# Second layer of a two-layer sequence model on one core: step sizes started ahead of the gates, row numbers counted on by ScalarE, and another order of work on the way to the sorted experts

## What is computed

```python
x_ssm, res = jnp.split(x @ W_in.T, 2, axis=-1)           # 512 and 512 channels
x_ssm = silu(causal_conv4(x_ssm) + b_conv)
dt = softplus(x_ssm @ W_dt.T + b_dt)                     # the step sizes
B_C = (x_ssm @ W_x.T)[..., 16:]                          # 16 states
def step(h, inp):                                        # 2048 steps, 512 x 16 states
    h = exp(dt_t[:, :, None] * A) * h + dt_t[:, :, None] * B_t[:, None, :] * x_t[:, :, None]
    return h, h.sum(-1) + D * x_t
y = scan(step) * silu(res)                               # silu(res): the gates
x = x + y @ W_out.T
# then two groups of 32 experts, top 2 of each: route, sort rows by expert,
# grouped SwiGLU, weighted sum back to the tokens
x = x + (group0(layernorm(x)) + group1(layernorm(x))) / 2
```

## Time and profile before

| | us |
|---|---|
| median of 3 runs | 4872.82 (4868.73 to 4875.76) |
| the profiled execution, whole | 4861.3 |
| its span, first to last instruction | 4859.5 |
| layer 1, from the first product L1456 (2499.1) to the end of the last (4167.0) | 1667.9 |
| from there to the first expert tile (4256.6) | 89.6 |
| experts, to the end | 602.9 |

### The profile page before, as it was taken

One profiled execution on the slowest core, in us unless ns is written; L12 is line 12 of the kernel. 1 busy time (PEld: TensorE's weight loads), 2 busy tenths in 40 slices (PEclk: granted clock), 3 DMA queues, 4 the chain that ended last, 5 costly groups with the idle time before them and its releaser, 6 DMA issues. The chain is left out here.

```text
span 4859.5 us, 59293 instructions
## 1 busy us (share of the span) xinstructions
PE 4278.9 (88%) x19350; PEld 2834.2 (58%) x19350; DVE 3722.3 (77%) x5916; ACT 2516.5 (52%) x4871; POOL 3037.6 (63%) x1970
## 2 busy tenths in 40 slices
PE   5689999999999999998988889888988888499993
PEld 1355555555556655565655566555655665388883
DVE  6887777778788878775149988888988898555676
ACT  1344334334333434433468777777777777155552
POOL 3455555555555545554158889888888888555552
PEclk7899999999999999999999999999999999699997
DMA  4233332333332333333112221111222111496787
GB/s 146 80 107 104 109 100 92 110 98 111 109 104 90 105 105 104 105 109 100 39 67 75 80 73 70 70 69 69 86 87 75 69 67 68 162 248 209 260 282 278
DMA packets 304193, 545.54 MB, mean 112 GB/s; under 512 B 31504, under 2 KB 148496, under 8 KB 294928
## 3 DMA queue, kind: packets, MB, share of 16 engines
q1 hardware_dynamic: 276240, 466.09, 29.5%
q0 software_dynamic: 27648, 75.67, 4.3%
HBM read 422.72 MB, written 118.92 MB: 111 GB/s over the span
## 5 line engine op out<-in xcount | busy, mean ns | idle before, releaser
L1456 POOL TENSOR_TENSOR c_dbx<-c_dtx,c_Brep 128x1024 f32<-128x1024 f32 x512 | 1200.5, 2362 | 167.8 <-DVE c_hs L1474 57.5
L876 POOL TENSOR_TENSOR a_kv<-a_rk,a_kv 128x512 f32<-128x512 f32 x512 | 807.7, 1589 | 402.9 <-DMA a_kv<-v_rows 402.6
L1474 DVE TENSOR_TENSOR_SCAN c_hs<-psum,c_carry,c_dbx 128x512 f32<-128x512 f32 x768 | 937.4, 1266 | 120.6 <-ACT psum L1463 68.0
L885 DVE TENSOR_TENSOR_SCAN a_S<-a_decay,a_carry,a_kv 128x513 f32<-128x513 f32 x512 | 795.1, 1553 | 185.4 <-POOL a_kv L876 94.4
L1463 ACT ACTIVATE psum<-c_dt,c_cols 128x512 f32<-128x512 f32 x1024 | 698.9, 689 | 402.6 <-DVE c_hs L1474 398.0
L802 POOL TENSOR_TENSOR a_hid_e<-a_hid_e,a_g_rep 128x512 f32<-128x512 f32 x256 | 386.7, 1513 | 773.3 <-ACT a_hid_e L791 596.9
L1490 PEld LDWEIGHTS psum<-ident,c_hs 128*128 128x128 f32 x4096 | 488.2, 144 | 394.5 <-DVE c_hs L1474 217.5
L1490 PE MATMUL psum<-ident,c_hs 128*128 128x128 f32 x4096 | 612.0, 282 | 114.1 <-DVE c_hs L1474 109.9
L891 DVE TENSOR_TENSOR a_prod<-a_rk,a_S 128x512 f32<-128x512 f32 x512 | 547.3, 1069 | 68.4 <-PE psum L907 68.4
L783 PE MATMUL psum<-a_W_down,a_hid_e 128*128 128x256 f32 x2304 | 552.0, 385 | 52.7 <-POOL a_hid_e L802 28.5
L207 PE MATMUL psum<-a_xT,a_W_up 128*128 128x512 f32 x1152 | 559.2, 615 | 15.1 <-ACT a_hid_e L791 15.0
(11 more groups left out here) (271 smaller groups left out, 6777.5 us busy)
## 6 DMA issues: line engine op xcount, KB each, us to landing
a_kv<-v_rows SPq DMA_DIRECT2D x512, 256.0 KB
a_g_rep<-g_rows SPq DMA_DIRECT2D x256, 256.0 KB, 3.9
c_Brep<-b_rows SPq DMA_DIRECT2D x64, 1024.0 KB, 4.7
d_xs<-sorted_rows SPq DMA_DIRECT2D x320, 128.5 KB
d_w<-results SPq DMA_DIRECT2D x64, 512.0 KB, 11.4
d_w<-in_d_experts SPq DMA_DIRECT2D x32, 768.0 KB, 8.8
sorted_rows<-d_zeros SPq DMA_DIRECT2D x66, 128.5 KB, 6.2
a_xa<-in_L_attn_x SPq DMA_DIRECT2D x16, 512.0 KB, 4.7
```

What stands on the lines that cost most here:

```text
L876: m_kv[g] = pool.mark(nc.gpsimd.tensor_tensor(kv[:, g % NV, 1:C + 1], rk[slot][:, 1, hb, :], kv[:, g % NV, 1:C + 1], ALU.mult))
L885: m_scan[q] = dve.mark(nc.vector.tensor_tensor_scan(S[:, q % NS, :], decay[cq % 2][:, hb, :], kv[:, q % NV, :], carry[:, sq_:sq_ + 1], ALU ...
L1456: m_dbx[g] = m_dbx[g + 1] = pool.mark(nc.gpsimd.tensor_tensor(dbx[:, r:r + 2, :], dtx[slot][:, e, :].unsqueeze(1).broadcast_to([P, 2, C]), ...
L1474: m_scan[q] = dve.mark(nc.vector.tensor_tensor_scan(hs[:, q % NR, :], psum[:, DA + q % ND, :], dbx[:, q % NX, :], first, ALU.mult, ALU.add))
```

## The change

1. `m_done["xs", c]` is set before the gates, so `sizes` and `prepare` may begin in front of gates and B rows. `step_size(e)` for `e >= 1` waits until the B rows are written.
2. The row number is counted on by ScalarE: before the first pick right after the norm in `after_scan`, between the picks in `sort_rows`; ScalarE then waits for the landing of the first eight DMAs. The pause before it is shorter by two yields, and one yield stands behind it.
3. In chunk 15, a new generator `turned_early` transposes the first three of four blocks of the gated result and multiplies them with `W_out`; `last_product` adds the fourth.
4. For the last chunk the normed rows are copied (`again`, ScalarE) with the second row number (VectorE), and the 16 DMAs are issued group by group without a wait between the picks.
5. The expert phase fetches all 16 weight blocks of group 0 first, has the plan's constants on a semaphore of their own, issues the second pad from ScalarE's queue, waits for the plan only after that, waits for each group's last rows alone, and issues the third pad behind the first six row tiles.

```diff
@@ main
             for e0 in range(0, EB, 2):
                 yield from inner(e0)
                 yield
+            m_done["xs", c] = list(m_xs.values())
...
             yield from gates(2)
             m_done["gate", c] = m_gate[TL - 1]
-            m_done["xs", c] = list(m_xs.values())
@@ sizes
             def step_size(e):
+                while e >= 1 and not is_done(("stored", c)):
+                    yield
@@ after_scan
-            marks = m_done["y", c] = yield from transposed(gate[slot], yT, EB, m, y_free)
...
+            if c < NCH - 1:
...
+            else:
+                products = yield from last_product(c)
...
+            if c >= 2:
+                m_done["row", c] = act.mark(nc.scalar.activation(xn_[:, :, D], xn_[:, :, D], ACT.Identity, bias=two_chunks[:, 0:1]))
...
+            if c == NCH - 1:
+                act.after(m_done["scanned", c][0], m_done["scanned", c][1])
+                dve.after(m_done["scanned", c][0])
+                m_done["copied", c] = [act.mark(nc.scalar.copy(again[:, t, 0:D], xn_[:, t, 0:D])) for t in range(TL)]
+                m_done["copied", c].append(dve.mark(nc.vector.tensor_scalar(again[:, :, D], token_row[:, :], float(c * C * TOP + 1), None, ALU.add)))
@@ new
+        def turned_early(c):
+            marks = m_done["turned", c] = []
+            for e in range(EB - 1):
+                while not is_done(("gated", c, e)):
+                    yield
...
+                    m = nc.tensor.transpose(bank[:, t * P:(t + 1) * P], gate[c % 2][:, t, e * P:(e + 1) * P], ident[:, :])
...
+            while not is_done(("placed", c - 1)):
+                yield
...
+                    for e in range(EB - 1):
+                        nc.tensor.matmul(bank[:, t * D:(t + 1) * D], pre[:, e, at:at + P], W_out[:, e, :], start=(t == 0 and e == 0), stop=False, skip_group_check=True)
+                    yield
+            m_done["begun", c] = True
@@ sort_rows
-            if c >= 2:
-                pool.engine.wait_ge(s_sorted[c % 2], c // 2 * per_chunk)
-                m_row = pool.mark(nc.gpsimd.tensor_tensor(route.xn[c % 2][:, :, D], route.xn[c % 2][:, :, D], two_chunks[:, :], ALU.add))
+            m_row = m_done["row", c]
+            if c == NCH - 1:
+                pool.after_alone(*m_done["placed", c], *m_done["copied", c], m_row)
+                for g in range(GR):
+                    for k in range(TOP):
+                        for t in range(TL):
...
             for k in range(TOP):
                 if k:
-                    yield from pause(POOL_LAG)
-                    pool.engine.wait_ge(s_sorted[c % 2], c // 2 * per_chunk + per_chunk // TOP)
-                    pool.after_alone(pool.mark(nc.gpsimd.tensor_tensor(route.xn[c % 2][:, :, D], route.xn[c % 2][:, :, D], ones[:, 0:TL], ALU.add)))
+                    yield from pause(POOL_LAG - 2)
+                    act.engine.wait_ge(s_sorted[c % 2], c // 2 * per_chunk + per_chunk // TOP)
+                    m_row = act.mark(nc.scalar.activation(route.xn[c % 2][:, :, D], route.xn[c % 2][:, :, D], ACT.Identity, bias=ones[:, 0:1]))
+                    yield
+                    pool.after_alone(m_row)
@@ sorted_experts_phase
-        EARLY = 6
+        nc.sync.dma_start(plan, I["d_plan"]).then_inc(s_plan, 16)
         for n in range(EARLY):
             fetch_weights(0, n)
...
-        nc.sync.dma_start(plan, I["d_plan"]).then_inc(s_load, 16)
-        for n in range(EARLY, E // 2):
-            fetch_weights(0, n)
...
-        sp.after(m_plan, m_pad, m_zeros)
-        for block in range(PADS):
-            pad(block)
-        for slot in range(2):
-            sp.engine.wait_ge(s_sorted[0][slot], s_sorted[1])
+        sp.after(m_pad, m_zeros)
+        act.after(m_pad, m_zeros)
+        pad(0)
+        pad(1, nc.scalar)
+        sp.after(m_plan)
+        for sorted_sem, count in route.sorted:
+            sp.engine.wait_ge(sorted_sem, count)
         for j in range(AHEAD):
             fetch_rows(j)
+        pad(PADS - 1)
```

More of the change, by code:

```diff
@@ L1007, in layer1_phase @@
         s_sorted = [sem(f"sorted{i}") for i in range(2)]
+        s_last = [sem(f"last_of_group{g}") for g in range(GR)]
         NR, NX, DA, ND = 8, 6, 3, 3
@@ new lines, in last_product @@
+        def last_product(c):
+            e = EB - 1
+            while not is_done(("begun", c)):
+                yield
+            i, bank = yield from G.claim(pe)
+            pe.after(m_done["gated", c, e])
+            for t in range(TL):
+                m = nc.tensor.transpose(bank[:, t * P:(t + 1) * P], gate[c % 2][:, t, e * P:(e + 1) * P], ident[:, :])
+            act.after(pe.mark(m))
+            m_y = G.freed[i] = act.mark(nc.scalar.copy(pre[:, e, 0:C], bank))
+            pe.after(m_y)
+            products = []
+            for half, (i, bank) in enumerate(m_done["products", c]):
+                for t in range(2):
+                    at = (2 * half + t) * P
+                    m = nc.tensor.matmul(bank[:, t * D:(t + 1) * D], pre[:, e, at:at + P], W_out[:, e, :], start=False, stop=(t == 1), skip_group_check=True)
+                products.append((i, bank, pe.mark(m)))
+            return products
@@ L1672, in sorted_experts_phase @@
         pe, act, dve, pool, sp = L.pe, L.act, L.dve, L.pool, L.sp
-        s_load, s_out = sem("load"), sem("out")
+        s_load, s_plan, s_out = sem("load"), sem("plan"), sem("out")
         s_w = [sem(f"w{i}") for i in range(E // BLOCK)]
```

83 lines of the change are left out of this document (56 added, 27 removed).

## The result

The changed kernel takes 4884.58 us (median of 19 runs, 4876.77 to 4899.60), the kernel before 4875.76 us (19 runs, 4868.73 to 4886.45). The ratio is 1.0019, with a 95% interval of 1.0011 to 1.0026: 0.2% slower, where 4803 us and 1.5% faster had been forecast. The profiled execution took 4880.2 us, its span is 4878.4.

The account below looks back on a forecast made before the run. GpSimd, VectorE and TensorE were each taken as 89% busy in the loop, with GpSimd waiting for dtx. Loop 43 us plus way 27 us, together 70, took 4861.3 to 4791.3; plus 11.5 for the median, 4803 us, range 4768 to 4848.

Parts of the forecast that it names:

- The order of the step sizes: Loop: setting xs ahead of the gates removes GpSimd's 3.8 us dtx wait, less 1.35; gain 2.4 us a chunk.
- TensorE's order changes, its work doesn't: Loop, step sizes moved ahead of gates: TensorE only gets another order of the same work; no cost given.
- drift by a step a chunk: Loop background: earlier preparation could spread the router and make the sort stream slip one step a chunk; no cost given.
- rival C: Loop: step sizes hold banks, gates delay exponentials, losing 4.2 us a chunk; 4905 us in all, chance 0.07.
- The row numbers: Loop: two additions a chunk move from GpSimd to ScalarE, hidden there; 1.86 us a chunk off GpSimd.
- The ceiling of 6.0 us: Loop: chunk 1, without sorting, takes 100.5 us, so unhindered GpSimd buys at most 6.0 us a chunk.
- Rival A: Loop: VectorE keeps what GpSimd gives, dtx waits return as c_hs waits; loop gain 10, 4836 us, chance 0.18.
- The way: Last product to first expert tile: gains of 29.7 us, less 3, make 27 us, between 18 and 31.
- Last product: Way: with three quarters done early, last gate product to last sum falls from 12.1 to 4.4 us; gain 7.7.
- places to first tile: Way: from rows placed to first expert tile, 39.8 us becomes 19 to 21; gain 20.
- The 3 us taken off for ScalarE's wait: Way: 3 us deducted for late early products and ScalarE waiting for chunk 14's scatters ahead of the router's exp.
- Nothing in them changed: Experts: 320 tiles follow shifted at an even pace, staying at 603 us.

Follow-up runs that it names:

- e1: Kernel before with only the early order: xs set ahead of the gates, later step sizes behind the B rows; 4886.83 us, ratio 1.0050.
- e4: Changed kernel with only the early order taken back, xs set behind the gates again; 4838.87 us, ratio 0.9945.
- e6: Changed kernel with step sizes and the next input allowed from step 50 instead of 38; 4856.96 us, ratio 0.9961.
- e7: e4 with the two pauses of a chunk's first step size cut to one yield each; 4845.27 us, ratio 0.9929.
- e2: Kernel before with only the row numbers moved from GpSimd to ScalarE; 4867.90 us, ratio 1.0014.
- e11: e4 with norm statistics of one token block in four used for all, output not the reference's; executed once, loop 1647.1 us.
- e12: e7 and e8 together: e4 with short pauses and the third pad issued early by ScalarE; 4827.84 us, ratio 0.9931.
- e8: e4 with the third pad issued on ScalarE's queue ahead of the row tiles; ratio 0.9935.
- e5: Changed kernel with the next input's preparation held until all four gates are written; 4869.69 us, ratio 0.9983.
- e14: Kernel before with four banks for the background and two for the scans' exponentials, instead of three each; ratio 1.0071.
- e13: Changed kernel with four banks for the background and two for the scans' exponentials, instead of three each; ratio 1.0061.

## Why the prediction was wrong

**The order of the step sizes** was the step that failed. It said that the 3.8 us a chunk of waiting for `dtx` go, less 1.35 for the two operations that come ahead, and put the new order of TensorE's queue at nothing. Term forecast: +2.4 us a chunk; measured -1.9 alone (e1) and -2.7 beside the row numbers (after against e4). The wait did go (52.8 to 15.9 us). What stood in its place are waits that the same move makes: VectorE for the ranks' product, 28.2 us in e1 and 56.6 in e6, 1.2 before; GpSimd's products for scans, 80.6 for 37.1 us (e1); ScalarE with the gates' table loaded, 3.31 us in chunk 9; and the drift. The error was to price a wait by its length on the engine that waits, without asking what the moved operations would stand in front of. e6 and e7 remove it with no gain in a middle chunk, each at the price of a new wait, so how much of the 2.4 us was ever there stays open.

**"TensorE's order changes, its work doesn't"** passed over its first half. The order put products of step sizes between those of gates (3522.82 to 3532.06 above) and ahead of the ranks. The second half is true of the work, but not of its time: nearly the same records took 24 us more, at a granted clock of 0.96 for 0.99. Of the 32.0 us by which chunks 2 to 14 are longer than in the earlier trace rows, TensorE's busy time has 24.1. How much of those lies on the path isn't shown; in the ten us from 3528.5 TensorE is busy throughout and VectorE waits 6.87 us for it.

**The drift** was named ("drift by a step a chunk") and the banks were called what decides, but then rival C was turned down with the sentence that a held bank "makes a background stream give its turn away, it doesn't stop a queue". True, and it is how the order comes to drift: a stream that gives its turn away is written later, and from there the operations of five streams meet in other places in every chunk. C got the mechanism in part, the bank and the exponential behind a pair of gates, and missed its form: 2.5 us a chunk in a cycle of seven, not 4.2 in one collision. It had 0.07; the 1.9 us from which it was to decide was passed.

**The row numbers** were right in what they cost GpSimd (e2: 19.0 us of idle time and the additions gone) and wrong in what that is worth: 0.26 us a chunk, or 0.45 without chunk 2, not three quarters of 1.86. (Three quarters of the forecast's 4.3 us a chunk are 3.2, and 45 us in all, where it wrote 3.1 and 43; nothing hangs on it.) The ceiling of 6.0 us taken from chunk 1 was read wrongly. Chunk 1 lacks 17 us of GpSimd's work, but TensorE, too, is busy 4.9 us less in it than in a mean chunk, 89.9 for 1232.33 / 13 = 94.8, at a clock of 1.00. Rival A, that VectorE keeps what GpSimd gives, was the nearest for this part and allowed 10 us for the loop; e4, the change without the order, has 3.2. In e2 the waits for `c_hs` do rise (54.2 us for 37.1), but those for `dtx`, which A had return as them, are still there (54.6).

**The way** was right in its three gains. Last product 8.0 us for 7.7 forecast; norm 1.9 for 2.0 (0.6 us between statistics and power, for 2.5); places to first tile 20.2 for 20. The 3 us taken off for ScalarE's wait were 4.8: from the norm's power to the router's first maximum 14.6 us for 9.9, with the 5.93 us for chunk 14's scatters in it. Sum 25.3 for 27.

**The experts** were wrong by a small term. "Nothing in them changed" left out that the pads, which stood ahead of the row tiles, now stand between them on SyncE's queue. It costs 5.7 us (e11 less e12) to 8.2 (e7 less e8). The rest of the 16.9 us needn't be the change's: e4 and e7 have the changed kernel's code there and take 606.7 and 618.8 us. The profiles of after and of e5 to e8 have two stalls of some 4 us, at tiles 122 and 230, that those of before, e1 to e4 and e11 to e14 don't have, and e5 to e8 were taken on one chip. On that chip the kernel before takes 4878.98 us, on the two others 4865.23 and 4866.22, so the stalls are probably there without the change too; no profile of before from it shows them. What makes them is open.

The sum by the profiles: loop +29.3, way -25.5, experts +16.9 and -1.8 ahead of the loop make +18.9. 8.8 us lie between the medians, so a part of the profiles' difference is that of the two executions. That the gain of the way and the loss of the loop nearly cancel is chance; nothing in the forecast says so.

## What to carry to other kernels

A wait has no price by its length alone. When work is moved forward to remove it, list on every engine's queue what the moved operations now stand in front of, and follow the freed engine to its next wait; and take a stretch without that engine's load as a ceiling only when the other engines' rows are the same there. Where background work shares a few banks by giving turns away, tabulate for several chunks at which step each operation is written; if the positions no longer repeat, the change isn't the one costed. And when transfers are moved off the critical wait, see what they now stand in front of on their queue.

## What the runs showed of the hardware

TensorE's clock was part of the time wherever waits had grown, with a drifting order (after, e1) and with a steady one (e13): after a wait of 2.30 us four matmul records of 512 columns took 3.62 us and soon after 1.88. In chunks 2 to 14 the granted clock was 0.99 (before, e2, e4, e7, e11), 0.98 (e6) and 0.96 (after, e1, e13, e14), and TensorE's busy time for nearly the same records 1226 to 1233 us in those down to 0.98 and 1247 to 1256 in the others. The experts took 600 to 607 us in the profiles of e1 to e4 and e11 to e14, from two chips, and 611 to 624 in those of e5 to e8, from a third, with the same instructions but for the order of the pads; a few us there were comparable on one chip only. The loops agreed within 0.8 us between chips.
